# The first feed-forward's gate and up products in one-pass 32-bit form, on activations split in two parts, with the first stage's order timed anew

## The reference, cut to what matters

```python
def ternary_quant(w_fp32, g=64): ...      # per group of 64: scale * round(w / scale) clipped to -1..1, in bf16
gate, up = split(x @ ternary_quant(w_gate_up).T)   # 256 -> 2 * 1024
h = silu(gate) * up
y = rms_norm(h) @ ternary_quant(w_proj).T           # 1024 -> 256
```

## Time and profile before

| | us |
|---|---|
| median of 3 runs (1619.8 to 1626.96) | 1621.21 |
| the profiled execution | 1618.92 |
| its span | 1617.1 |

### The profile page before, as it was taken

One profiled execution on the slowest core, in us unless ns is written; L12 is line 12 of the kernel. 1 busy time (PEld: TensorE's weight loads), 2 busy tenths in 40 slices (PEclk: granted clock), 3 DMA queues, 4 the chain that ended last, 5 costly groups with the idle time before them and its releaser, 6 DMA issues. The chain is left out here.

```text
span 1617.1 us, 35674 instructions
## 1 busy us (share of the span) xinstructions
PE 1443.5 (89%) x13996; PEld 1048.8 (65%) x13996; DVE 1057.4 (65%) x2150; ACT 849.9 (53%) x1728; POOL 530.1 (33%) x558
## 2 busy tenths in 40 slices
PE   4478989899999989999999989999899977888998
PEld 3246767676776767777676776776666744554855
DVE  5997586676858677685777768677634364563344
ACT  3456555555665565566556656565444216665311
POOL 2952233232323323232342333323234356440100
PEclk9689999999999999999999999999999988999899
DMA  4121111120111112011120211011210120000200
GB/s 162 21 76 34 31 25 41 25 44 9 34 32 25 42 25 44 9 36 31 24 54 12 44 22 24 28 25 31 86 66 1 50 76 1 2 1 12 68 0 27
DMA packets 142485, 56.39 MB, mean 35 GB/s; under 512 B 109776, under 2 KB 134992, under 8 KB 142064
## 3 DMA queue, kind: packets, MB, share of 16 engines
q1 hardware_dynamic: 133424, 48.20, 13.0%
q10 hardware_dynamic: 8896, 5.91, 1.2%
HBM read 37.11 MB, written 16.97 MB: 33 GB/s over the span
## 5 line engine op out<-in xcount | busy, mean ns | idle before, releaser
L1137 POOL TENSOR_TENSOR og<-og,sz 128x256 f32<-128x256 f32 x128 | 92.7, 728 | 570.7 <-DVE og L1080 344.8
L530 PE MATMUL banks<-wv,xT 128*128 128x512 f32 x256 | 132.8, 657 | 6.8 <-DVE Yv L927 5.9
L914 ACT ACTIVATE junk<-og 128x512 f32<-128x512 f32 x64 | 40.4, 631 | 176.7 <-POOL og L1137 176.7
L674 PE MATMUL banks<-wz,xT 128*128 128x256 f32 x512 | 124.1, 384 | 9.0 <-DVE yacc L1100 9.0
L927 DVE SCALAR_TENSOR_TENSOR Yv<-banks,cwall,Yv 128x511 f32<-128x511 f32 (+2 forms) x192 | 131.1, 739 | 0.7 <-ACT Yv L767 0.7
L745 PE MATMUL banks<-wo,oT 128*128 128x256 f32 x512 | 128.9, 396 | 0.6 <-ACT oT L919 0.6
L530 PE MATMUL banks<-wqk,xT 128*128 128x512 f32 x256 | 122.0, 611 | 0.6 <-DVE Yk L927 0.6
L674 PEld LDWEIGHTS banks<-wz,xT 128*128 128x128 f32 x512 | 94.6, 190 | 31.3 <-issue 19.3
L745 PEld LDWEIGHTS banks<-wo,oT 128*128 128x128 f32 x512 | 96.0, 195 | 19.9 <-issue 6.2
L1100 DVE TENSOR_TENSOR yacc<-yacc,banks 128x512 f32<-128x512 f32 x64 | 43.8, 685 | 94.4 <-PE banks L745 94.0
L1144 POOL TENSOR_TENSOR rn<-ss,c_half 128x4 f32<-128x4 f32 x64 | 64.9, 1014 | 102.1 <-DVE ss L1094 101.9
(11 more groups left out here) (364 smaller groups left out, 3620.7 us busy)
## 6 DMA issues: line engine op xcount, KB each, us to landing
cm_d<-CM SPq DMA_DIRECT2D x32, 256.0 KB, 4.3
wqk<-in_L_attn_W_qkvz SPq DMA_DIRECT2D x8, 512.0 KB, 5.0
wv<-in_L_attn_W_qkvz SPq DMA_DIRECT2D x8, 512.0 KB, 4.5
wz<-in_L_attn_W_qkvz SPq DMA_DIRECT2D x16, 256.0 KB, 2.9
wo<-in_L_attn_W_out SPq DMA_DIRECT2D x16, 256.0 KB, 3.1
blk<-cm_d SPq DMA_DIRECT2D x128, 16.0 KB, 1.8
t_d<-tb SPq DMA_DIRECT2D x16, 128.0 KB, 1.7
Td<-t_d SPq DMA_DIRECT2D x128, 16.0 KB, 1.9
```

The source lines that it names most:

```text
L530: ins = pe.matmul(bank[b][:, :], xT[:, d, b * S + of_batch, :], w[:, d, :], start=(d == 0), stop=(d == KD - 1))
L674: ins = pe.matmul(bank[7][:, b * 256:(b + 1) * 256], xT[:, d, b * S + q, :], wz[:, d, :], start=(d == 0), stop=(d == KD - 1))
L1137: pool.tensor_tensor(og[:, n, :, :], og[:, n, :, :], sz[q % 2][:, b, :].rearrange("p (h d) -> p h d", h=VR), ALU.mult).then_inc(s["osz"].s ...
```

## The change

The gate and up products take x in two parts, both in the type float32r. `pool_parts` makes them on POOL for each batch, 4 instructions in all, into buffers that are free by then: `GL` and `GR` for batch 0, `Tf` and `P4` for batch 1. A unit has 8 products in place of 4. The weights stay where they were, with the buffers named anew in the type float32r; their loads are the same. PE waits for the parts at units 0 and 8. All due times (`TURN`, `FSTEP`, `AT`, `FIRST`, `FINAL`, `START`) are other numbers.

```diff
-TURN = 69.87
-FSTEP = 6.96
+TURN = 70.09
+FSTEP = 7.01
...
-    up_f = [line(wqk).rearrange("p (k f) -> p k f", k=KD)[:, k, :] for k in range(KD)] + [line(Yk[1]), line(kt[1])]
+    gate_r = rounded("f0_gate", "wqk", [P, KD, FF])
+    up_r = [rounded(f"f0_up{d}", where, [P, FF]) for d, where in enumerate(("Yk1", "kt1"))]
+    up_f = [gate_r[:, k, :] for k in range(KD)] + [t[:, :] for t in up_r]
+    f0x = [[rounded(f"f0_x_{part}{b}", where, [P, KD, S, P]) for b, where in enumerate(homes)] for part, homes in (("hi", ("GL", "Tf")), ("lo", ("GR", "P4")))]
...
+            if f == 0:
+                pe.wait_ge(*s["f0xhi"](b))
+                pe.wait_ge(*s["f0xlo"](b))
             for i in range(2):
                 for d in range(KD):
-                    ins = pe.matmul(pair[n % 2][:, i, :], up_f[2 * i + d][:, f * P:(f + 1) * P], xT[:, d, b * S:(b + 1) * S, :], start=(d == 0), stop=(d == KD - 1))
+                    for u in range(2):
+                        ins = pe.matmul(pair[n % 2][:, i, :], up_f[2 * i + d][:, f * P:(f + 1) * P], f0x[u][b][:, d, :, :], start=(d + u == 0), stop=(d + u == KD))
...
+    def pool_parts(pool):
+        for b in range(B):
+            yield START[f"f0x{b}"]
+            if b == 0:
+                pool.wait_ge(*s["Ep"](3, LAST))
+            else:
+                pool.wait_ge(*s["U64p"](1, LAST))
+            hi, lo, x = f0x[0][b], f0x[1][b], xT[:, :, b * S:(b + 1) * S, :]
+            pool.tensor_copy(hi[:, :, :, :], x).then_inc(s["f0xhi"].sem, 1)
+            pool.wait_ge(*s["f0xhi"](b))
+            yield START[f"f0x{b}"] + 2.0
+            pool.tensor_tensor(lo[:, :, :, :], x, hi[:, :, :, :].bitcast(F32), ALU.subtract).then_inc(s["f0xlo"].sem, 1)
```

More of the change, by code:

```diff
@@ L337 @@
 AT = {
[10 rows of a table removed]
-    "wout1": -4.41, "y": 12.07, "RECUR": 93.04, "STEP": 8.73, "OUT": 22.27,
[10 rows of a table added]
+    "y": 12.09, "RECUR": 92.32, "STEP": 8.69, "OUT": 21.55,
 }
 FIRST = {
[11 rows of a table removed]
[11 rows of a table added]
 }
 FINAL = {
[10 rows of a table removed]
-    "wout1": -157.95, "y": 13.14, "RECUR": 92.63, "STEP": 8.9, "OUT": 20.51,
[10 rows of a table added]
+    "wout1": -125.14, "y": 11.47, "RECUR": 92.88, "STEP": 8.71, "OUT": 23.12,
 }
 START = {
[4 rows of a table removed]
-    "fill1": 71.63, "cwp": -151.33, "cwe": -72.97,
[4 rows of a table added]
+    "fill1": 71.83, "cwp": -132.8, "cwe": -70.02,
 }
@@ L393, in gdn, with placed @@
         "qinA": -1, "qinB": -1, "qinC": -1, "qin1": -1, "qin2": -2, "qcast": 6, "qthr": 24, "qcmp": 10, "qpool": 24, "qlow": 4, "qtp": 10, "qtc": 10, "qout0": -5, "qout1": -5, "abs1": 4, "sum1": 1, "thr1": 3,
-        "f0wg": -1, "f0wu": -2, "f0w2": -2, "f0hid": 32, "f0act": 16, "f0h": 16, "f0sq": 16, "f0acc": 14, "f0ss": 1, "f0ms": 1, "f0r": 1, "f0dn": 4, "f0y": 8} | PREP)
+        "f0wg": -1, "f0wu": -2, "f0w2": -2, "f0hid": 32, "f0xhi": 2, "f0xlo": 2, "f0act": 16, "f0h": 16, "f0sq": 16, "f0acc": 14, "f0ss": 1, "f0ms": 1, "f0r": 1, "f0dn": 4, "f0y": 8} | PREP)
     tab, cw, xT, yacc = m["tab"], m["cwall"], m["xT"], m["yacc"]
-    many = lambda n, count, shape: [sb(f"{n}{i}", shape) for i in range(count)]
-    wqk, wv = sb("wqk", [P, 2, KD, BLK]), sb("wv", [P, KD, BLK])
+    base = {}
+    def placed(n, shape, dt=F32):
+        base[n] = nc.sbuf_base
+        return sb(n, shape, dt)
+    rounded = lambda n, where, shape: nc.alloc_sbuf_tensor_at(n, shape, F32R, offset=base[where])
+    many = lambda n, count, shape: [placed(f"{n}{i}", shape) for i in range(count)]
+    wqk, wv = placed("wqk", [P, 2, KD, BLK]), sb("wv", [P, KD, BLK])
     wz, wo = sb("wz", [P, KD, VR * DH]), many("wo", 2, [P, VR, D])
-    GL, GR = sb("GL", [6, HC, P], BF16), sb("GR", [6, HC, P], BF16)
+    GL, GR = placed("GL", [6, HC, P], BF16), placed("GR", [6, HC, P], BF16)
     Yk, Yq, Yv = many("Yk", 3, [P, B, T]), many("Yq", 2, [P, B, T]), sb("Yv", [P, VR, B, T])
@@ L402, in gdn @@
     E, CM, A = sb("E", [P, VR, NT, P]), sb("CM", [P, VR, NT, P]), many("A", 2, [P, VR, NT, P])
-    Td, Ud, P2, Tf, P4 = (sb(n, [P, HC, w]) for n, w in (("Td", C), ("Ud", C), ("P2", C), ("Tf", 2 * C), ("P4", 2 * C)))
+    Td, Ud, P2, Tf, P4 = (placed(n, [P, HC, w]) for n, w in (("Td", C), ("Ud", C), ("P2", C), ("Tf", 2 * C), ("P4", 2 * C)))
     UB = many("UB", 2, [P, HC, P])
@@ L1312, in sp_forward @@
         sp.wait_ge(*s["proj"](3, LAST))
-        sp.dma_start(line(wqk).rearrange("p (k f) -> p k f", k=KD), m["up_d"][:, :, 0:FF]).then_inc(s["f0wg"].sem, 16)
+        sp.dma_start(gate_r[:, :, :].bitcast(F32), m["up_d"][:, :, 0:FF]).then_inc(s["f0wg"].sem, 16)
         sp.wait_ge(*s["KSp"](5, LAST - 2))
-        sp.dma_start(line(Yk[1]), m["up_d"][:, 0, FF:2 * FF]).then_inc(s["f0wu"].sem, 16)
+        sp.dma_start(up_r[0][:, :].bitcast(F32), m["up_d"][:, 0, FF:2 * FF]).then_inc(s["f0wu"].sem, 16)
         sp.wait_ge(*s["SU"](5, LAST - 2))
-        sp.dma_start(line(kt[1]), m["up_d"][:, 1, FF:2 * FF]).then_inc(s["f0wu"].sem, 16)
+        sp.dma_start(up_r[1][:, :].bitcast(F32), m["up_d"][:, 1, FF:2 * FF]).then_inc(s["f0wu"].sem, 16)
         sp.wait_ge(*s["nqs"](0, LAST))
@@ L1436, in on_gpsimd @@
     def on_gpsimd(pool):
-        streams(pool, (pool_key, pool_inverse, pool_recur, pool_finish), (start["pool"], pool_fill, pool_ternary), (pool_forward,))
+        streams(pool, (pool_key, pool_inverse, pool_recur, pool_finish), (start["pool"], pool_fill, pool_ternary), (pool_parts, pool_forward))
     def on_scalar(act):
```

## The result

| | before | changed |
|---|---|---|
| median of the runs taken together, us | 1620.51 (1618.15 to 1626.96, 4 runs) | 1600.29 (1599.84 to 1605.08, 4 runs) |
| span of the profiled execution, us | 1617.1 | 1598.7 |

A second measurement, further down, gave 0.9901 [0.9881, 0.9921]. The prediction was 1596, in a range of 1582 to 1609. The time is in it, but the parts of its sum come out otherwise.

The account below looks back on a forecast made before the run. PE was taken to bound the first stage. The terms -25.5 + 1.5 - 2.6 + 3 - 2 + 1 gave -24.6 us against 1618.92, so 1594.3, or 1596 as a median, in a range of 1582 to 1609.

Parts of the forecast that it names:

- What bounds: First stage: PE sets its end, so work taken from PE moves the end equally if other engines' chains keep up.
- The products: Feed-forward units on PE: 16 units go from 3.43 to 1.84 us each, -25.5 us.
- The splits: Casts and subtractions on POOL, 7.5 us: they can hold DVE, PE's fillers cover most, +1.5 us, between 0 and 7.5.
- The start: Head of the kernel: x loads ahead of the gate weights, copies to `xT` start earlier, -2.6 us, between 0 and -5.
- A turn in the middle: 14 middle turns under the new order: code waits fall, new waits come, together +3 us, bounds -16.6 to +19.
- rival 1: Middle turns get shorter: code stall goes, DVE's delay is covered, -13 in place of +3, 1580 us, chance 0.18.
- +0.9 a turn: Each middle turn, behind TU16: gate z waits for DVE's `yacc`, 4.7 us of work against PE's 3.85.
- The last turn: Last turn: larger products between P16 and TU16 cover part of the 4.23 us code stall, -2 us, between 0 and -5.5.
- The tail: Behind the last unit: POOL's last additions queue and PE's sums of squares wait, +1 us, between 0.5 and 2.5.
- Number 2: Last recurrence binds with short units: each of the last 8 lanes gives back 1.5 us, +12, 1608 us, chance 0.10.
- number 4: Gate z behind `yacc` in 14 turns: new waits pull the clock down, 41 us more, 1633 us, chance 0.03.

Follow-up runs that it names:

- e3: The changed kernel, new order and splits kept, with the units' products in the 32-bit form as before: 1.0032 to the kernel before, 1626 us.
- e1: The changed kernel with all due-time tables of the kernel before, splits still due as in the change: 0.9899 to the kernel before, 1605 us.
- e2: The kernel before with the changed kernel's due times, products in the 32-bit form, no splits: 1.0020 to the kernel before, 1624 us.
- e10: The changed kernel with P16 put directly ahead of TU16 again in the middle turns: 1.0135 to the kernel before, 1643 us.

## Why the prediction was right, and where its steps were not

- **What bounds.** Right: PE sets the first stage's end, and its work taken out counts whole (23.1 us in length, 25.8 between e3 and the changed kernel).
- **The products, -25.5.** Over by 2.4: I took 0.23 us for all 8 products, but the first of a unit takes 0.31 to 0.42. Layer 1's pair of rows stands in the middle of a run and can't show that; the first pair behind a wait there, from 1334.44 to 1335.01, takes 0.57 us, not 0.46.
- **The splits, +1.5.** The mechanism was right and the size too small: 4.1 us. One of two splits paid in full, with 2.4 us and a spell of low clock. I wrote that PE's fillers cover most; at batch 0's split there is no filler between `yacc` and z. For batch 1's the executions with and without it show the same waits (0.63 us for P at L647).
- **The start, -2.6.** Failed, and with the wrong sign: +7.2. The step was "its order is almost unchanged, so a shift at the head is carried on". I checked that for the preparation and not for turn 0, where the new order brings turn 1's projections later and leaves DVE with 1.43 us of work in 10. The old order reaches TU16 of turn 1 at 168.9 and 172.0 us, the new one at 175.4 to 180.2 in eleven executions, of which 1.8 us are work that stands ahead of it now. So the new order is shown as the cause, by e1 and e2; that it is these projections is read from two traces. The tables of turn 0 and of the middle wait for one another, so one alone was not tried.
- **A turn in the middle, +3.** It came out as -9.4, near rival 1 (its -13) and in part by its mechanism, DVE's delay that is covered. The term that failed is "+0.9 a turn" for z behind `yacc`: such waits were there before, 6.8 us, and fell to 2.3. Code waits went from TU16 as said (15.4 to 1.8 us), but P16 took up half of that (7.7 to 15.2), up to 4.4 us with a slow clock behind, which was in no case. The sum also put at nothing, without a reason, the waits for `E` and `Td`, 13.1 us that fell to 0.7, and new ones for `og` and `sq`, 8.6 us.
- **The last turn, -2.** Failed: the wait went to P16 and is 3.3 us there, in other executions up to 5.2. With z and og waiting longer (4.41 and 2.01 us for 1.73 and 1.36), the order costs 7.0 us in that stretch (5.1 with the usual wait for code), where -2 and the tail's +1 were forecast.
- **The tail, +1.** Half of it came: the wait for POOL is 1.22 us against 0.77. I had expected 1.5 to 2.
- **The rivals.** Number 2, a binding recurrence, is refuted for the changed kernel and true in part of e1: there 6.1 us of such waits appear, of the 12 that it named. Waits that pull the clock down turn after turn, as in number 4, did not occur in the change but did in e10, at 39 us.

So that the total was right to 0.3% is luck in part: errors of 8 to 12 us in three stretches offset each other.

## What to carry to other kernels

When a change comes with a new order, check the sum stretch by stretch: a good total can hold several wrong terms. Put work on GpSimd beside VectorE instructions that read PSUM, not beside those with two SBUF operands, and look at the instruction of 0.2 us as well as at the long ones. Keep weight loads out of the moment at which TensorE runs through its shortest instructions, and before moving a run of them by one place, look at who produces what both neighbours need.

## What was not expected of the hardware

- A wait of PE for code in a run of small products lasts up to 2.8 us where at most 0.5 MB is loaded beside it and up to 5.2 us with 1.5 MB or more (348 GB/s in 864 to 868 us of the changed kernel). PE goes on 1.2 to 1.6 us behind the end of the packet in all 163 cases. The page counts 113 packets and 1.85 MB on the instruction queue, 16 KB each. The Trainium skill, Advanced Engine Details, section "ISA Cache", gives 16 KB, 256 instructions, as the size of such a line; the packets agree. Which of these waits occur differs from one execution to the next; how much of the 5 to 10 us by which executions of one kernel differ here comes from them was not measured.
- Waits of 1.26, 0.68 and 1.28 us within 7 us in e10 came with a granted clock of 0.80 and 0.77 in the 8 us from 1046 us on; single waits of 0.46 us for V, and one of 1.14 us for code in the kernel before, left it at 1.00.
- The first product behind other work takes 0.31 or 0.42 us in the one-pass form, the following ones 0.23.
